# Routed experts of a two-layer vision tower: the first expert stage in units of two 64-slot halves on array quarters, and the last two units of both stages carried to the tokens by one-hot products

## The reference

```python
# first: top 1 of 8 experts, hidden 512
out = out + where(max_ind == e, silu(x @ w1[e]) * (x @ w2[e]) @ w3[e], 0)
out = out.astype(bfloat16) * max_prob
# second: top 2 of 8 experts, hidden 768
h = silu(xf @ Wg[e].T) * (xf @ Wu[e].T)
out = out + h @ Wd[e].T * w_e[:, None]
```

## Time and profile before

| what | value |
|---|---|
| time, three runs | 406.29 us median (405.89 to 407.03) |
| the profiled execution, its own time | 409.78 us |
| its span, first to last instruction | 408.0 us |
| PE busy | 348.6 us (85%) |
| DVE, ACT, POOL busy | 184.0, 134.8, 104.5 us |
| matmul instructions on PE | 2758 |
| moved by DMA | 59.51 MB |

### The profile page before, as it was taken

One profiled execution on the slowest core, in us unless ns is written; L12 is line 12 of the kernel. 1 busy time (PEld: TensorE's weight loads), 2 busy tenths in 40 slices (PEclk: granted clock), 3 DMA queues, 4 the chain that ended last, 5 costly groups with the idle time before them and its releaser, 6 DMA issues.

```text
span 408.0 us, 7081 instructions
## 1 busy us (share of the span) xinstructions
PE 348.6 (85%) x2758; PEld 291.5 (71%) x2758; DVE 184.0 (45%) x474; ACT 134.8 (33%) x278; POOL 104.5 (26%) x133
## 2 busy tenths in 40 slices
PE   4999946989788999966896987888899999999970
PEld 1999923567667999962465654575799999999960
DVE  2786793996552222216398555266422212121213
ACT  2997311444303222321387042321321212121210
POOL 3299542000023443122032202000423232211120
PEclk9999976987776999996999798995999999999995
DMA  7933239930371795007003999002249999999204
GB/s 237 345 84 75 63 81 253 271 93 2 108 202 52 203 247 124 15 16 195 0 0 77 258 252 259 28 0 67 60 105 291 277 254 255 258 251 249 65 31 130
DMA packets 28707, 59.51 MB, mean 146 GB/s; under 512 B 10081, under 2 KB 15234, under 8 KB 28674
## 3 DMA queue, kind: packets, MB, share of 16 engines
q1 hardware_dynamic: 26274, 53.48, 50.1%
q0 software_dynamic: 2400, 5.57, 5.0%
HBM read 55.12 MB, written 3.92 MB: 145 GB/s over the span
## 4 chain that ended last, share of the span: by engine, by line
PE 60%; DVE 17%; ACT 8%; DMA 8%; issue 4%; SPq 2%; POOL 0%; DVEq 0%; POOLq 0%; ACTq 0%
PE ps L1604 15%; PE ps L1629 12%; PE ps L1616 9%; PE ps L1412 4%; PE ps L1345 4%; DMA xw<-in_xw 3%; DVE cv L1264 3%; ACT xp L661 2%; PE ps L1418 2%; DVE xn L974 2%; DVE xn L950 2%; PE ps L1467 2%; SPq L349 2%; PE ps L1547 2%; DMA yg<-token_y 2%
## 5 line engine op out<-in xcount | busy, mean ns | idle before, releaser
L1604 PE MATMUL ps<-xgt,wup 128*128 128x128 f32 x576 | 70.9, 280 | 2.3 <-DVE ht L1196 1.8
L1604 PEld LDWEIGHTS ps<-xgt,wup 128*128 128x128 f32 x576 | 69.4, 196 | 2.8 <-issue 2.8
L1196 DVE TENSOR_TENSOR ht<-sg,ps 128x384 f32<-128x384 f32 (+1 forms) x56 | 27.7, 497 | 77.5 <-ACT sg L774 75.5
L597 POOL DMA_INDIRECT xg<-token_x,src_id x26 | 25.3, 972 | 145.5 <-DVE src_id L1166 95.3
L1629 PE MATMUL ps<-wdn,ht 128*128 128x192 f32 x288 | 53.8, 335 | 0.0
L1345 PE MATMUL ps<-busy 128*128 128x512 bf16 x108 | 38.9, 486 | 11.1 <-DVE h L1211 6.6
L1629 PEld LDWEIGHTS ps<-wdn,ht 128*128 128x128 f32 x288 | 46.1, 190 | 3.1
L604 POOL DMA_INDIRECT token_y<-ysb,row_id x28 | 27.5, 981 | 67.6 <-ACT ysb L781 67.6
L774 ACT ACTIVATE sg<-ps 128x384 f32<-128x384 f32 (+1 forms) x56 | 24.8, 444 | 49.9 <-PE ps L1616 49.1
L1353 PE MATMUL ps<-weff,xp 128*128 128x193 f32 x240 | 39.9, 327 | 1.6 <-ACT xp L661 1.6
L1353 PEld LDWEIGHTS ps<-weff,xp 128*128 128x128 f32 x240 | 39.2, 190 | 2.4 <-issue 2.4
(11 more groups left out here) (295 smaller groups left out, 511.0 us busy)
## 6 DMA issues: line engine op xcount, KB each, us to landing
wup<-in_m_w SPq DMA_DIRECT2D x16, 576.0 KB, 8.5
wup<-in_m_w SPq DMA_DIRECT2D x48, 192.0 KB, 9.4
wdn<-in_m_w SPq DMA_DIRECT2D x16, 576.0 KB, 11.4
wup<-in_m_w SPq DMA_DIRECT2D x12, 384.0 KB, 6.1
wup<-in_m_w SPq DMA_DIRECT2D x36, 128.0 KB, 6.6
wdn<-in_m_w SPq DMA_DIRECT2D x12, 384.0 KB, 9.3
xw<-in_xw SPq DMA_DIRECT2D x2, 784.0 KB, 12.3
wall<-in_w_sh SPq DMA_DIRECT2D x2, 768.0 KB, 10.2
```

Source lines behind the costliest of these rows:

```text
L597: g.indirect_dma_start(xg[:, j, :], None, token_x[m], bass.IndirectOffsetOnAxis(ap=src_id[:, j:j + 1], axis=0))\
L1196: v.tensor_tensor(ht[:, j % 2, s, 0:half], sg[:, s, 0:half], ps[:, 2 * s + 1, 0:half], ALU.mult)\
L1604: mm(ps[:, 2 * s + g, c * P:c * P + P], up[:, col:col + P], xgt[:, 0, j * P:j * P + P], start=(c == 0), stop=False)
```

## The change

**Stage one in halves.** The unit of work stays 128 slots, but is now two halves of 64 slots, each with an expert of its own. There are (576 + 8*63) // 64 = 16 halves (`M1_HALVES`), 8 units. The weights of a half are still one expert's, so 16 are loaded instead of 12, in nine buffers instead of eight. The 192 numbers of a token are now three blocks of 64 rows (`KB`), gate weights in rows 0 to 63, up weights in rows 64 to 127, so each load is nine DMAs instead of five. Every product of the stage is 64 rows by 64 output rows, a quarter of the array, and quarters (row half g, column half i) follow one another in the program: `up_half` has 48 of 64 columns for each half, `down_pair` 16 of 192 columns for each unit, `across` (which takes the place of the transposes) 12. The gate side of `down` and the up side land in two banks, and are added by ACT (`y_low`) and DVE (`both_rows`).

**The last two units.** The results of the last two units (`KEPT`) of each stage aren't scattered. DVE makes a one-hot matrix of slots against tokens for each (`last_units`; in stage two with the gates in it), PE transposes it (`kept_across`), and `combine` multiplies it by the unit's result into one PSUM bank for each tile of tokens. In stage one `combine` also adds the rows read back (an identity product of `yg`), and DVE's `routed` reads PSUM. In stage two a last DVE addition takes PSUM to `h`. Since the rows of the last units are no longer written, SP first fills `token_y` with zeros.

```diff
-M1_TILES = (T + E * (P - 1)) // P
+H = 64
+M1_HALVES = (T + E * (H - 1)) // H
+M1_TILES = (M1_HALVES + 1) // 2
+KB = D // H
-M1_BUFS, M2_BUFS = 8, 6
-W_LOADS = 5
+M1_BUFS, M2_BUFS = 9, 6
+W_LOADS = (9, 5)
+KEPT = 2
@@ SP: loads of an expert, later experts, results
+                if m == 0:
+                    pieces = []
+                    for g in range(2):
+                        at, n = H * g, slice(g * hid, (g + 1) * hid)
+                        pieces += [(up[at:at + H, 0:hid], w12[0:H, 0, n]),
+                                   (up[at:at + DH - H, hid:2 * hid], w12[H:DH, 0, n]),
+                                   (up[at + DH - H:at + H, hid:2 * hid], w12[0:lo, 1, n]),
+                                   (up[at:at + H, 2 * hid:3 * hid], w12[lo:DH, 1, n])]
...
-                    sp.wait_ge(S["p_y"], j - r["bufs"] + 1 + r["before"])
+                    last = j - r["bufs"]
+                    if last >= 0:
+                        sp.wait_ge(S["p_y"], (last // 2 if m == 0 else last) + 1 + r["before"])
...
-                    sp.wait_ge(d_y[b], 8 * (r["n"] + r["before"]))
+                    sp.wait_ge(d_y[b], 8 * (r["n"] - KEPT) + scattered(m))
...
+            zeros = (busy[:, 0:D], busy[:].bitcast(F32)[:, 0:D])
+            for m in range(2):
+                for k in range(MOE[m]["k"]):
+                    y = token_y[m][k * TPAD:(k + 1) * TPAD, :].rearrange("(t p) d -> p t d", p=P)
+                    load(y, zeros[m].unsqueeze(1).broadcast_to([P, TT, D]), "d_zero")
@@ POOL: no scatter of the last two units
-                    if j >= 1:
+                    if j == 0:
+                        pool.wait_ge(S["d_zero"], 48)
+                    elif j <= n - KEPT:
                         scatter(j - 1)
-                scatter(n - 1)
@@ DVE
+                def both_rows(j):
+                    dve.wait_ge(S["a_yh"], j + 1)
+                    if j >= 2:
+                        dve.wait_ge(d_y[j % 2], j // 2 * 16)
+                    v.tensor_tensor(ysb[m][:, j % 2, :], y_low[:], ps[:, 5, 0:D], ALU.add).then_inc(S["v_y"], 1)
...
-                dve.wait_ge(S["d_yg"], 32)
-                v.scalar_tensor_tensor(out=h[0:rows, t, :], in0=yg[0][0:rows, 0, t, :],
+                dve.wait_ge(S["p_cmb"], t + 1)
+                v.scalar_tensor_tensor(out=h[0:rows, t, :], in0=ps[0:rows, TILE_BANK[t], 0:D],
...
+                dve.wait_ge(S["p_cmb"], TT + t + 1)
+                dve.wait_ge(S["v_h"], 5 * TT + t + 1)
+                v.tensor_tensor(h[0:rows, t, :], h[0:rows, t, :], ps[0:rows, TILE_BANK[t], 0:D], ALU.add)\
@@ PE
+                def up_half(j, s):
+                    t = 2 * j + s
...
+                    if j >= 1:
+                        pe.wait_ge(S["v_ht"], 2 * (j - 1) + s + 1)
+                    for c in range(hid // P):
+                        for k in range(KB):
+                            for g in range(2):
+                                rows = slice(H * g, H * g + H)
+                                for i in range(2):
+                                    col = c * P + H * i
+                                    ins = mm(ps[H * i:H * i + H, 2 * s + g, c * H:c * H + H], up[rows, k, col:col + H],
+                                             xh[rows, t, k, :], start=(k == 0), stop=(k == KB - 1))
...
+                def down_pair(j):
+                    pe.wait_ge(S["v_ht"], 2 * j + 2)
+                    if j >= 1:
+                        pe.wait_ge(S["a_yh"], j)
+                        pe.wait_ge(S["v_y"], j)
...
+                    for c in range(hid // P):
+                        for g in range(2):
+                            rows = slice(H * g, H * g + H)
+                            for i in range(2):
+                                dn = wbuf[0][(2 * j + i) % M1_BUFS][1]
+                                ins = mm(ps[H * i:H * i + H, 4 + g, 0:D], ht[rows, j % 2, i, c * H:c * H + H],
+                                         dn[rows, c, :], start=(c == 0), stop=(c == hid // P - 1))
...
+                def combine():
+                    pe.wait_ge(S["a_oh"], 1 if m_ == 0 else 1 + KEPT)
+                    pe.wait_ge(S["v_oh2"], 1 if m_ == 0 else 1 + KEPT)
+                    pe.wait_ge(S["v_y" if m_ == 0 else "a_y"], n)
+                    if m_ == 0:
+                        pe.wait_ge(S["d_yg"], 32)
+                    for t in range(TT):
+                        k = P if t < TT - 1 else LAST
+                        o = ps[0:k, TILE_BANK[t], 0:D]
+                        if m_ == 0:
+                            mm(o, identb[0:k, 0:k], yg[0][0:k, 0, t, :], start=True, stop=False)
+                        for l in range(KEPT):
+                            ins = mm(o, kept_at[m_][:, l, t * P:t * P + k], ysb[m_][:, (n - KEPT + l) % 2, :],
+                                     start=(m_ == 1 and l == 0), stop=(l == KEPT - 1))
...
+                if m_ == 0:
+                    for j in range(n):
+                        up_half(j, 0)
+                        if j >= 1:
+                            down_pair(j - 1)
+                        if j + 1 < n:
+                            across(j + 1)
+                        else:
+                            for l in range(KEPT):
+                                kept_across(l)
+                        up_half(j, 1)
+                    down_pair(n - 1)
+                    combine()
+                    return
```

More of the change, by code:

```diff
@@ L1076, in experts @@
                 r = MOE[m]
-                n, half, before, K = r["n"], r["hid"] // 2, r["before"], r["k"]
+                n, half, before, K, L = r["n"], r["hid"] // 2, r["before"], r["k"], r["slots"]
+                over = (M1_HALVES if m == 0 else n) - E
                 i_ln = 2 if m == 0 else 5
@@ L1334, in _ @@
                                            op0=ALU.mult, op1=ALU.add).then_inc(S["v_h"], 1)
+            for t in range(TT):
+                rows = P if t < TT - 1 else LAST
+                dve.wait_ge(S["p_cmb"], TT + t + 1)
+                dve.wait_ge(S["v_h"], 5 * TT + t + 1)
+                v.tensor_tensor(h[0:rows, t, :], h[0:rows, t, :], ps[0:rows, TILE_BANK[t], 0:D], ALU.add)\
+                    .then_inc(S["v_h"], 1)
         @block.tensor
@@ L1631, in down, with across @@
                     ins.then_inc(S["p_y"], 1)
+                def across(j):
+                    pe.wait_ge(S[f"d_xg{j}"], rows_gathered(0, j))
+                    pe.wait_ge(S["a_gt"], j)
+                    pe.wait_ge(S["a_f1" if j == 1 else "v_gt"], max(j - 1, 1))
+                    for c in range(KB):
+                        for s in range(2):
+                            rows = slice(H * s, H * s + H)
+                            for i in range(2):
+                                ins = mm(ps[H * i:H * i + H, 6 + s, c * H:c * H + H], xg[rows, j, H * c:H * c + H],
+                                         ident[rows, rows], start=True, stop=True)
+                    ins.then_inc(S["p_gt"], 2)
```

218 lines of the change are left out of this document (169 added, 49 removed).

## The result

The changed kernel takes 416.71 us (median of 4, 413.45 to 417.15), the kernel before 406.66 on the same chip (4 runs, 405.89 to 407.24): ratio 1.023, 95% interval 1.018 to 1.029. Forecast were 399.4 us (392.5 to 405.0) and a gain with a chance of 0.81. By the ratio it is slower by 9.4 us; the medians are 10.05 apart. An execution that took over 1.5% more than the fastest of its kernel counts in the medians of this document, and not in its ratios and intervals.

The account below looks back on a forecast made before the run. Stage one was taken as PE-bound, with SP's weight-load issues the next limit. Stage one's -2.4 and stage two's -4.5 made -6.9: profiled 409.8 becomes 402.9, which stands 3.5 above the median, so 399.4 us (392.5 to 405.0).

Parts of the forecast that it names:

- So SP sets it: Stage one's late weight loads: SP's issues, not the transfers, pace the last seven halves; last issue starts at 172.3 us.
- The start: Start of stage one: PE, at half clock after the gather at 124.0, ends the first down pair near 131.7 us.
- The price of a half: SP's cost of one half's nine DMAs in stage one, with the lead before them: 5.87 us.
- From last issue to landing: Stage one's last weight load: 4 us, since pieces issued slower than they drain leave no backlog.
- Behind the landing: Stage one after its last weights: products, silu, down pair, copy, addition and first combine product, 7.7 us at half clock.
- Matmuls at 0.014 us four abreast: Stage one's quarter products: four quarters of the array work at once, 0.014 us a matmul of 64 columns.
- PE's part of a unit: PE's work on one stage-one unit, two halves and a down pair: some 4.4 us.
- Rival (b): Stage one quarters paid by the instruction, 0.033 to 0.036 us a matmul; 412.0 us at 0.036; chance 0.10.
- Rival (c): Stage one's small weight pieces drain slower than issued, 7.5 us a half; total 410.8 us; chance 0.08.
- Rival (a): Stage one weights come sooner, SP paying 5.1 us a half without the 0.74 lead; midway 395.3 us; chance 0.23.
- Stage two: End of stage two: one-hot products replace scatter, load and late additions; end at 400.7 instead of 405.16, -4.5 us.
- The end of stage one: Reckoned together with the halves: DVE's first addition after stage one at 184.0 instead of 186.35, -2.4 us.

Follow-up runs that it names:

- plain_rows: no_reload with POOL's indirect gathers and scatters in stage one made plain DMAs to and from fixed rows; result differs; 405.37 us, timed once.
- nine_pieces: Kernel before, its 12 tiles and products kept, each expert loaded in nine DMAs of the changed kernel's shapes instead of five; 409.71 us, timed once.
- wide: Changed kernel with two quarters of 64 output rows joined into one up product of 128, half as many instructions; 416.52 us, ratio 1.019.
- half_products: Changed kernel computing only one of the two column halves of each up product, same loads; result differs; 410.62 us, timed once.
- no_reload: Changed kernel without the loads of halves 9 to 15, buffers keeping the first nine halves' weights; result differs; 402.19 us, timed once.
- wide_one_piece: Changed kernel with up products of 128 output rows and each half loaded in two DMAs instead of nine; 408.90 us, ratio 0.999.
- tail_two: Kernel before with the one-hot end in stage two alone, 128-slot tiles in both stages; 400.56 us, ratio 0.984; repeated 401.96 us, 0.987.
- tail_both: Kernel before with the one-hot end in both stages, 128-slot tiles in both; 398.65 us, ratio 0.978; repeated 397.25 us, 0.976.
- one_piece: Changed kernel with up weights laid out by the host as the buffer holds them, two DMAs a half instead of nine; 413.32 us, ratio 1.018.

## Why the prediction was wrong

**Which step failed.** "So SP sets it: the last issue starts at 131.7 + 7 x 5.87 - 0.45 = 172.3" put the last issue 14.6 us too early (186.94). Its terms:

- The start. Forecast 132.4, measured 137.65: +5.2. PE needed 7.5 us for the first half's products (121.60 to 129.1), held back while POOL had four gathers in a row; plain_rows took that away. From there to the end of the first down pair, chain of waits in after:

```profile
129.24 0.53 PE ps L1776 x20
...
129.88 2.56 PE ps L1800 x96
132.44 1.49 issue
133.93 1.57 PE ps L1800 x92
...
135.55 1.34 PE ps L1819 x31
```

That is 7.65 us, 1.49 of it at a block, where the forecast had 7.7 (124.0 to 131.7). So all of the 5.2 lies before 129.24: 1.6 is the stage starting later, and the rest, 3.6, is the first half, which the chain of waits shows as the last to end there, and not the gather.

- The price of a half, 5.87 forecast, 7.34 measured: +9.4 to the last issue. 0.26 of each is the pieces' own (nine_pieces 6.13). The other 1.2 go with the fetches: 11 in the 49.3 us from 137.65 to 186.94 are 1.64 a half, so 0.74 us each. By that wide, with 6 in 45.1, should have 6.13 + 0.89 x 0.74 = 6.8, and has 6.7; half_products, with 6 in its six halves, should have 6.9, and has 6.9.
- From last issue to landing 4 forecast, 6.88 measured: +2.9. "Pieces that are issued slower than they drain leave none" didn't hold; why isn't settled. The two result loads and the next stage's weights are issued from 0.6 us behind it on, but so they are in wide, where the same landing took 3.51; in half_products it took 4.99.
- Behind the landing 7.7 forecast, 6.82 measured: -0.9. Half clock was right for the up products (2.85 for 96), and the down pair ran at full clock (1.57 for 32).

14.6 + 2.9 - 0.9 = 16.6 = 200.64 - 184.0.

**The step under it that would have failed anyway.** Matmuls at 0.014 us four abreast are nearly right inside a burst (92 in 1.57 us in after at 133.93, at full clock: 0.017 each, 0.015 from start to start), and that is what I multiplied. Over a stage they aren't: 254 matmuls and weight loads take 3.6 to 4.0 us from the end of one gap to the end of the next in no_reload (from 147 us on, at full clock) and in plain_rows, 0.015 us an instruction, 0.030 a matmul with its weight load. PE's part of a unit is 7.45 us, not 4.4. Rival (b) had 0.033 to 0.036 "paid by the instruction" and named the 3,000 more instructions to be fetched, at a chance of 0.10, and the point from which the change loses, 0.0325. Its price is nearly that measured; its mechanism, a weight load that is waited for, is wrong, and no_reload with 186.5 shows PE's stage ending where before's does, not 5 to 10 us later. The 12.7 us by which stage one is longer in after need the loads on top: without reloads they are gone.
The Trainium skill (Runtime: NRT & Kernel Launch, "Instruction fetch mechanics") says that a sequencer gets its instructions in blocks of 16 KB, 256 instructions, and that crossing a block is "mostly hidden". The trace agrees with the block (0.56 MB in 34 packets, gaps 254 rows apart) and, at this rate, not with hidden: gaps of up to 1.9 us without weight loads, up to 3.4 with them. In the kernel before it was hidden, at 88 instructions in 4.4 us.

**Rival (c)** is false: DMA share in stage one was 0.40 to 0.68 between 135 and 185, and nine_pieces loads the same pieces at no loss. Its 7.5 us a half was near the measured 7.34 by luck. The figure of the Trainium skill behind it (DMA: Bandwidth & Descriptors, "Bandwidth", 0.95 us for 64 KB) is of DMAs issued from GpSimd and isn't what binds here: nine pieces undisturbed take 6.13 us, and SP's issues, not the transfers, set that.
**Rival (a)** had no part: SP paid its lead of 0.7 to 0.8 us before each half. Its counter-argument, that the DMAs allow no less than 4.9 us a half, is false as a limit (332 GB/s in wide_one_piece).

**Stage two** was right: -4.5 forecast, -4.7 in after, -4.8 in tail_two, where it stands alone. `combine` took 3.65 us (3.6), ten transposes 1.28 (1.2). The rival that part of it came from the changed first stage is out.

**The end of stage one** had been reckoned with the halves in one sum, and so its worth was hidden: with 128-slot tiles, where PE and not the loads is the last, it is worth some 5 us in the profile. So of the change's +9.4 us, the two one-hot ends bring about -9 to -10 (tail_both) and the halves cost some 18 to 19, a difference of two kernels and not a run of its own. The profiles split it: stage one takes 64.8 us in tail_both, 71.4 in no_reload and 84.5 in after. About 6.6 us are thus PE with quarters and all weights there, and 13.1 come with the seven loads.

## What to carry to other kernels

A rate read inside a burst of short products is no rate of a stage: count the instructions, and compare them with what the engine gets supplied, here 256 in 3.6 to 4.0 us. That matters as soon as a matmul with its weight load takes less than 0.03 us. A fetch is paid by others as well, here by each DMA issue beside it. And where a change has two ideas, forecast and time each alone: here one was worth 2.3% and the other cost some 4.5%.

## What the runs showed of the hardware that I had not expected

- PE's stream stalls at blocks of 256 instructions when its products would eat one in less than the 3.6 to 4.0 us that no_reload and plain_rows show; at 304 rows in 7.3 us (wide_one_piece) there is no such gap. The gap ends 2.2 to 2.8 us after the block's packet starts, and is longest (2.7 to 3.4 us, four times) in one_piece, with its dense weight loads.
- While POOL issues four indirect DMAs in a row, PE gets 3 to 8 instructions in each 0.6 to 0.7 us (after, no_reload). With plain DMAs in their place (plain_rows) 96 matmuls run through in 1.63 us.
- A DMA issue of SP that falls beside an instruction packet takes 0.84 to 1.36 us instead of 0.3 to 0.5 in after, eleven times out of eleven; in wide four of six packets have such an issue.
- A float32 matmul with 64 rows, 128 output rows and 64 columns costs 0.057 us, over three times one with 64 output rows in a burst (0.017), and hardly less than one with 128 columns (0.068).
- The same weights come at 332 GB/s in two DMAs a half laid out as the buffer holds them (wide_one_piece), and at 240 in five as before.
